# Attention's output product in three fp32r passes, placed ahead of a slot's other projections

## The chip, the cores and the metric

The kernel runs on one core of a Trainium2 chip. The metric is the device time of one execution in microseconds (us). Before the change it is 1490.11 us, the median of three runs (1487.82 to 1490.38).

## What is computed

Eight sequences of 512 rows, 128 columns each, go through a layer in three steps, each on a layer norm of the rows: half a feed-forward, attention, half a feed-forward.

```python
x = x + 0.5 * _L0_ffn_ref(_layernorm(x), ...)
x = x + _L0_attn_ref(_layernorm(x), Wq, Wk, Wv, Wo)
x = x + 0.5 * _L0_ffn_ref(_layernorm(x), ...)
```

Attention has 16 heads of 64 columns, causal:

```python
q = (x @ Wq).reshape(B, S, H, dk)
k = (x @ Wk).reshape(B, S, H, dk)
v = (x @ Wv).reshape(B, S, H, dv)
scores = jnp.einsum('bqhd,bkhd->bhqk', q / math.sqrt(dk), k)
scores = scores + jnp.where(causal, 0.0, -jnp.inf)
attn = jax.nn.softmax(scores, axis=-1)
out = jnp.einsum('bhqk,bkhd->bqhd', attn, v).reshape(B, S, H * dv)
return x + out @ Wo
```

The feed-forward routes each row to 6 of 32 experts (through the best 2 of 4 groups), adds one of 16 anchor experts and a shared one; the kernel computes all hidden columns and scales them by the routing weights.

## The kernel before, in words

**Stages.** A chunk is one sequence: 512 rows, `CH`. The program is `ffn(0)`, `attention()`, `ffn(NC)`, with `NC` = 8 chunks in each. Each engine has its own instruction list, written out by hand in the order in which it stands; semaphores join them. No scheduler moves anything.

**Feed-forward.** A chunk has `HT` = 21 tiles of 128 hidden columns. For each, TensorE makes gate and up (`gate_up`, three fp32r passes each), ScalarE the SiLU (L748), VectorE gate times up (L1124) and the scaling by the routing row (L1156, both inputs in SBUF), and three tiles later TensorE adds the tile's down product in fp32 (L391). `gate_up` of tile j waits for `gated_done` of tile j-3.

**Three passes.** `mm3` (L195 to L199) makes a product of two fp32 operands from their rounded high parts and the rounded rests: high by high, high by low, low by high. The high part comes from a ScalarE copy into an fp32r tile, the low part from a subtraction: on VectorE for activations (`part_lo`), on GpSimd for the weights (`split_lo`, and L1347 for the attention weights `aw`). An ordinary fp32 product is one `matmul` call that the trace records as two matmul instructions.

**Attention.** A pair is two heads; a block has `HP` = 8 pairs, so there are 64 pairs and 64 slots (`attn_slot`). The slot of pair p holds on TensorE, in this order: transposes of the probabilities of pair p-1 (`probT` groups 1 and 2) around the first two score groups of pair p+1; the keys' projection of pair p+2 (`project(..., 1, psA)`), a tile of values (`project_values`), the output product of pair p-2 (`project_out`, L532, fp32), the queries' projection of pair p+2 (`project(..., 0, psA)`); the third score group; the first transposes of pair p; and the product of probabilities and values of pair p-1 (`attend`, L519), again into `psA`. Keys, queries and the attended sums share the PSUM bank `psA`. So the queries' projection waits for `k_lo`, the end of VectorE's low part of the keys, and `attend` waits for `q_lo`.

**ScalarE in a slot:** copy of the attended sums (`ctx_copy`, L825), two copies of transposed probabilities (L814), keys' high part (L781), exponentials of score group 0 (L803), values' copy (L789), queries' high part (L781), exponentials of groups 1 and 2.

**VectorE in a slot:** copy of transposes (L1227), reciprocals (L1220), row maxima of groups 0 and 1 (L1212), keys' low part (L1205), queries' low part (L1201), row maxima of group 2, copy of transposes. GpSimd scales the probabilities after the reciprocals (L1358).

**Slots that carry more.** In blocks 1 to 7: p = 1 has `outT_copy` on ScalarE ahead of the queries' high part and `rows_out` on TensorE after `attend`; p = 2 has `add_out` (L1233) on VectorE between reciprocals and row maxima, and `rows_stats` (L946, L948) between the keys' and the queries' low part; p = 3 has `rows_mean` (L954 to L960) there. The "special" slots (`special_slot`: p = 4 of blocks 0 to 6, and two around the start of the last block) transpose the next block's rows into `psA` first (`a_prep`), and there the keys' projection goes to `psT[:, 1, :]` behind the values, so that nothing waits for `k_lo` ahead of the queries. The output product of a block's pair 0 waits for `out_added`, which `add_out` of the block before sets.

**Start and weights.** SP's queue loads `small` (identity, masks, constants; 992 columns), the first rows, gate weights and bias (L287 to L290), then expert weights. VectorE begins when `consts_loaded` has all three. The attention weights come during the first feed-forward; ScalarE rounds three of them (`attn_split_hi`, tiles 11 to 13 of its last chunk), GpSimd takes the rests, and the first projection waits for `aw_lo`, 3.

## Time and profile before

| what | value |
|---|---|
| median of three runs | 1490.11 us |
| the profiled execution, its own time | 1488.8 us |
| its span, first to last instruction | 1487.0 us |
| granted TensorE clock, mean of the core | 0.998 |
| TensorE busy | 1436.2 us, 97% |
| VectorE busy | 1082.8 us, 73% |
| ScalarE busy | 806.6 us, 54% |
| GpSimd busy | 294.5 us, 20% |
| chain of waits, share by engine | PE 90%, DVE 5%, ACT 3% |
| output product L532 | 128 matmul records of 592 ns |

PE is TensorE's matmuls, PEld its weight loads, DVE is VectorE, ACT is ScalarE, POOL is GpSimd, SP the engine that issues the DMAs. The profiler models the end of a matmul with its pipeline, so consecutive ones overlap in the records: what a matmul costs is read from its start to the next one's start, and not from its duration. The chain of waits follows the work that ended last back to the start; the timeline lists instructions with their start in us from the span's start. Attention runs from about 432 to 1090 us.

### The profile page before, as it was taken

The numbers are of one execution on the slowest core, as the hardware profiler recorded it, in microseconds if no ns is written. First come the engines' busy times: TensorE is split into PE (matmuls) and PEld (weight loads), VectorE is DVE, ScalarE is ACT, GpSimd is POOL, SyncE is SP. The second block draws the span as 40 slices with busy tenths as digits, with TensorE's granted clock in tenths as the row PEclk, the third lists the DMA queues.
The fourth block names the chain that finished last, engine by engine and source line by source line (L and its number), as shares of the span: only waits on it lengthen the run. The fifth ranks groups of instructions, "written<-read, shape, count | busy, mean of one in ns | idle before, by whom it ended". The sixth has DMA issues, their size and how long they took to land.

```text
span 1487.0 us, 28766 instructions
## 1 busy us (share of the span) xinstructions
PE 1436.2 (97%) x9664; PEld 959.0 (64%) x9664; DVE 1082.8 (73%) x2421; ACT 806.6 (54%) x1907; POOL 294.5 (20%) x589
## 2 busy tenths in 40 slices
PE   2999999999988999999999999999899999999998
PEld 1666666666655666666666666666566666666665
DVE  6977877787676666676767677767767877687775
ACT  2443334333356777777777777787644334433422
POOL 2100000000013444434443444344400000000000
PEclk9999999999999999999999999999999999999999
DMA  5343333333310000000000000000033333333332
GB/s 185 128 166 110 104 116 102 111 101 112 114 44 1 2 2 2 2 2 1 2 2 2 2 2 2 1 2 2 2 108 103 117 119 113 104 116 119 111 113 85
DMA packets 58854, 97.80 MB, mean 66 GB/s; under 512 B 6144, under 2 KB 15360, under 8 KB 58752
## 3 DMA queue, kind: packets, MB, share of 16 engines
q1 hardware_dynamic: 58752, 96.44, 20.4%
q8 instruction: 63, 1.03, 0.3%
q14 instruction: 39, 0.32, 0.1%
HBM read 92.75 MB, written 3.67 MB: 65 GB/s over the span
## 4 chain that ended last, share of the span: by engine, by line
PE 90%; DVE 5%; ACT 3%; issue 1%; DMA 1%; POOL 0%; SPq 0%; POOLq 0%; ACTq 0%; DVEq 0%
PE banks L391 19%; PE banks L197 14%; PE banks L199 13%; PE banks L198 13%; PE banks L519 9%; PE banks L484 9%; PE banks L505 5%; PE banks L532 3%; PE banks L494 2%; PE banks L353 2%; ACT work L803 1%; PE banks L363 1%; DVE work L1156 1%; DVE work L1124 1%; DVE q_lo L1201 1%
## 5 line engine op out<-in xcount | busy, mean ns | idle before, releaser
L748 ACT ACTIVATE work<-banks 128x512 f32<-128x512 f32 x336 | 200.6, 598 | 459.1 <-PE banks L199 439.4
L391 PE MATMUL banks<-work,wd 128*128 128x512 f32 x672 | 343.0, 593 | 0.3 <-DVE work L1156 0.3
L1124 DVE TENSOR_TENSOR work<-banks,work 128x512 f32<-128x512 f32 x336 | 231.9, 690 | 150.9 <-ACT work L748 146.0
L803 ACT ACTIVATE work<-banks,nmax 128x512 f32<-128x512 f32 (+3 forms) x512 | 264.0, 527 | 39.0 <-DVE nmax L1212 39.0
L1358 POOL TENSOR_SCALAR work<-work,rrec 128x512 f32<-128x512 f32 (+3 forms) x512 | 262.9, 536 | 0.0
L197 PE MATMUL banks<-xT_hi,wg_hi 128*128 (+1 forms) x336 | 248.3, 739 | 0.1
L1156 DVE TENSOR_TENSOR work<-work 128x512 f32<-128x512 f32 x320 | 226.0, 706 | 15.1 <-DVE work L1124 9.5
L1212 DVE TENSOR_REDUCE nmax<-banks 128x2 f32<-128x1024 f32 (+3 forms) x256 | 198.9, 819 | 10.8 <-PE banks L494 6.6
L1227 DVE COPY stage<-banks 128x1024 f32<-128x1024 f32 (+1 forms) x128 | 122.1, 954 | 59.0 <-PE banks L505 58.9
L391 PEld LDWEIGHTS banks<-work,wd 128*128 128x128 f32 x672 | 126.1, 189 | 34.1 <-DVE work L1156 2.7
L198 PE MATMUL banks<-xT_lo,wg_hi 128*128 (+1 forms) x336 | 133.0, 396 | 0.0
L197 PE MATMUL banks<-xT_hi,wu_hi 128*128 (+1 forms) x336 | 133.0, 396 | 0.0
L199 PE MATMUL banks<-xT_hi,wu_lo 128*128 (+1 forms) x336 | 133.0, 396 | 0.0
L198 PE MATMUL banks<-xT_lo,wu_hi 128*128 (+1 forms) x336 | 132.9, 396 | 0.0
L199 PE MATMUL banks<-xT_hi,wg_lo 128*128 (+1 forms) x336 | 132.9, 396 | 0.0
L814 ACT ACTIVATE stage<-banks 128x512 f32<-128x512 f32 x128 | 76.6, 598 | 86.7 <-PE banks L505 84.6
L505 PE MATMUL banks<-small,work 64*128 64x64 f32 x2560 | 114.7, 225 | 4.3 <-DVE stage L1227 2.7
L505 PEld LDWEIGHTS banks<-small,work 64*128 64x128 f32 x2560 | 98.3, 138 | 17.5 <-issue 16.0
L197 PEld LDWEIGHTS banks<-xT_hi,wg_hi 128*128 128x128 f32 x336 | 64.0, 191 | 67.5 <-issue 64.2
L1201 DVE SCALAR_TENSOR_TENSOR q_lo<-banks,q_hi 128x512 fp32r<-128x512 f32 x64 | 44.3, 693 | 86.8 <-ACT q_hi L781 86.8
L198 PEld LDWEIGHTS banks<-xT_lo,wg_hi 128*128 128x128 f32 x336 | 64.2, 191 | 65.3 <-issue 65.0
L803 ACT ACTIVATION_READ_ACCUMULATOR work<-banks,nmax 128x1 f32 x512 | 105.3, 206 | 0.0
(130 smaller groups left out, 2186.3 us busy)
## 6 DMA issues: line engine op xcount, KB each, us to landing
work<-cw_rows SPq DMA_DIRECT2D x320, 256.0 KB, 3.1
x<-in_x SPq DMA_DIRECT2D x8, 256.0 KB, 6.7
out_rows<-x SPq DMA_DIRECT2D x8, 256.0 KB, 2.2
cw_rows<-cwT SPq DMA_DIRECT2D x16, 96.0 KB, 1.9
stage<-in_w_gate SPq DMA_DIRECT2D x3, 448.0 KB, 5.5
stage<-in_w_up SPq DMA_DIRECT2D x3, 448.0 KB, 6.1
wd<-in_w_down SPq DMA_DIRECT2D x3, 448.0 KB, 6.8
stage<-in_wq SPq DMA_DIRECT2D x1, 512.0 KB, 4.0
```

What stands on the lines that cost most here:

```text
L197: pe.matmul(o, w[0], m[0], start=start, stop=False, skip_group_check=True)
L198: pe.matmul(o, w[0], m[1], start=False, stop=False, skip_group_check=True)
L199: return pe.matmul(o, w[1], m[0], start=False, stop=stop, skip_group_check=True)
L391: pe.matmul(psY, wd[:, j * P:(j + 1) * P], z[part_slot(j)], start=j == 0, stop=j == HT - 1, skip_group_check=True).then_inc(s["down_ps"], 1)
L484: pe.matmul(ps[:, i, o:o + w], qk[0][a][r, p % 2, qb * P:(qb + 1) * P], qk[1][c][r, p % 2, 0:w], start=qb != 0 and k == 0, stop=False, ski ...
L505: m = pe.transpose(psT[:, h, k * DK:(k + 1) * DK], prob[r, p % 2, i, o:o + P], ident[r, h * DK:(h + 1) * DK])
L748: nc.scalar.activation(silu[j % 2], psG[j % 3], ACT.Silu) \
L803: m = nc.scalar.activation(prob[:, p % 2, i, o:o + w], ps[:, i, so:so + w], ACT.Exp, bias=nmax[:, p % 2, i, qb:qb + 1], accum_out=rsum[:, ...
L1124: tt(gated[j % 3], psU[j % 3], silu[j % 2], ALU.mult) \
L1156: tt(z[part_slot(j)], gated[j % 3], spread[:, j % NSPREAD, :], ALU.mult) \
L1212: m = nc.vector.tensor_reduce(nmax[:, p % 2, :, qb], ps[:, :, o:o + (qb + 1) * P], AX.X, ALU.max, negate=True)
L1358: nc.gpsimd.tensor_scalar(t, t, rrec[:, par, i, qb:qb + 1], 1.0, ALU.mult, ALU.mult) \
```

## The change

Four edits. The output weights are a fourth member of `attn_w` and `aw`, rounded and split like the others, and the output product is an `mm3` of them with the attended sums, whose high part ScalarE's copy writes and whose low part is a new VectorE subtraction, `ctx_low`. On TensorE the output product stands ahead of keys and values in every slot; the keys' projection goes to `psT[:, 1, :]` in every slot. On ScalarE the exponentials of group 0 stand ahead of the keys' high part. And `small` is loaded in two parts, the masks' 768 columns as a DMA of their own behind the bias.

```diff
-SMALL = 7 * P + E + TB * G * G
+SMALL = P + E + TB * G * G
...
-            sp.dma_start(small[:, :], small_in).then_inc(s["consts_loaded"], 16)
+            sp.dma_start(small[:, :], small_in[:, 0:SMALL]).then_inc(s["consts_loaded"], 16)
...
+            sp.dma_start(half_f32, small_in[:, SMALL:]).then_inc(s["half_loaded"], 16)
...
-            sp.dma_start(wo[:, :].rearrange("p (j d) -> p j d", d=P),
+            sp.dma_start(attn_w[:, 3, :].rearrange("p (j d) -> p j d", d=P),
...
-                    pe.wait_ge(s["aw_lo"], 3)
+                    pe.wait_ge(s["aw_lo"], 4)
...
             def project_out(b, p, first):
                 n = pair(b, p)
-                pe.wait_ge(s["ctx_sb"], n + 1)
+                pe.wait_ge(s["ctx_lo"], n + 1)
...
-                pe.matmul(psO, wo[:, p * P:(p + 1) * P], ctx_sum[:, :], start=p == 0, stop=p == HP - 1,
-                          skip_group_check=True).then_inc(s["out_ps"], 1)
+                c = slice(p * P, (p + 1) * P)
+                mm3(pe, psO, [w[:, 3, c] for w in aw], [t[:, :] for t in ctx_parts], p == 0, p == HP - 1) \
+                    .then_inc(s["out_ps"], 1)
...
-                    if have_q and special:
+                    if have_q:
                         pe.wait_ge(s["k_lo"], n + 3)
...
-                if have_q and not special:
+                if not (first and p < 2):
+                    bo, po = ahead(b, p, -2)
+                    project_out(bo, po, first)
+                if have_q:
+                    if first and p == 0:
+                        pe.wait_ge(s["q_lo"], 2)
+                    else:
+                        pe.wait_ge(s["pT_act"], 2 * n)
                     if p2 == 0:
                         pe.wait_ge(s["a_xT_lo"], b2 + 1)
-                    project(b2, p2, 1, psA)
+                    project(b2, p2, 1, psT[:, 1, :])
...
                 elif have_q:
-                    pe.wait_ge(s["k_lo"], n + 3)
+                    sums_out()
...
-                    if std_n == 3 and j >= AW_SLOT and j - AW_SLOT < 3:
+                    if std_n == 3 and j >= AW_SLOT and j - AW_SLOT < 4:
                         attn_split_hi(j - AW_SLOT)
...
-                nc.scalar.activation(ctx_sum[:, :], psA, ACT.Copy).then_inc(s["ctx_sb"], 1)
+                nc.scalar.activation(ctx_parts[0][:, :], psA, ACT.Copy).then_inc(s["ctx_hi"], 1)
...
-                if have_q and not special:
-                    part_hi(*ahead(b, p, 2), 1, False)
                 if have_s:
                     exp(*ahead(b, p, 1), 0, first and p == 0)
+                if have_q:
+                    part_hi(*ahead(b, p, 2), 1, False)
...
+            def ctx_low(b, p):
+                n = pair(b, p)
+                dve.wait_ge(s["ctx_hi"], n + 1)
+                tt(ctx_parts[1][:, :], psA, f32(ctx_parts[0][:, :]), ALU.subtract).then_inc(s["ctx_lo"], 1)
...
                     pT_copy(*ahead(b, p, -1), 1, first and p < 3)
+                if not (first and p < 2):
+                    ctx_low(*ahead(b, p, -2))
                 row_rec(b, p)
...
-            for w in range(3):
+            for w in range(4):
                 pool.wait_ge(s["aw_hi"], w + 1)
```

`sums_out` is the wait for the copy of the attended sums (now `ctx_lo` of pair n-2), which stood ahead of the keys in a plain slot and now stands ahead of the queries.

TensorE, the middle of a plain slot (block 4), before. In `xT_hi,aw_hi` the names are the moving and stationary operands in either order; the first three rows are the keys, the next three the values:

```order
L197 MATMUL banks<-xT_hi,aw_hi 128x512
L198 MATMUL banks<-xT_lo,aw_hi 128x512
L199 MATMUL banks<-xT_hi,aw_lo 128x512
L197 MATMUL banks<-aw_hi,xT_hi 128x512
L198 MATMUL banks<-aw_lo,xT_hi 128x512
L199 MATMUL banks<-aw_hi,xT_lo 128x512
L532 MATMUL banks<-ctx_sum,wo 128x512
L197 MATMUL banks<-xT_hi,aw_hi 128x512
L198 MATMUL banks<-xT_lo,aw_hi 128x512
L199 MATMUL banks<-xT_hi,aw_lo 128x512
L484 MATMUL banks<-k_hi,q_hi 128x256 x2
```

The same place in the changed kernel:

```order
L197 MATMUL banks<-ctx_hi,aw_hi 128x512
L198 MATMUL banks<-ctx_lo,aw_hi 128x512
L199 MATMUL banks<-ctx_hi,aw_lo 128x512
L197 MATMUL banks<-xT_hi,aw_hi 128x512
L198 MATMUL banks<-xT_lo,aw_hi 128x512
L199 MATMUL banks<-xT_hi,aw_lo 128x512
L197 MATMUL banks<-aw_hi,xT_hi 128x512
L198 MATMUL banks<-aw_lo,xT_hi 128x512
L199 MATMUL banks<-aw_hi,xT_lo 128x512
L197 MATMUL banks<-xT_hi,aw_hi 128x512
L198 MATMUL banks<-xT_lo,aw_hi 128x512
L199 MATMUL banks<-xT_hi,aw_lo 128x512
```

The output product has moved from behind the values to the front, as three passes in place of one call, and queries follow values at once.

ScalarE, a plain slot from the copy of the attended sums to the queries' high part, before:

```order
L825 ACTIVATE ctx_sum<-banks 128x512
L814 ACTIVATE stage<-banks 128x8x64
L814 ACTIVATE stage<-banks 128x512
L781 ACTIVATE k_hi<-banks 128x512
L803 ACTIVATE work,rsum<-banks,nmax 128x512 x2
L789 ACTIVATE work<-banks 128x512
L781 ACTIVATE q_hi<-banks 128x512
```

and in the changed kernel:

```order
L834 ACTIVATE ctx_hi<-banks 128x512
L823 ACTIVATE stage<-banks 128x8x64
L823 ACTIVATE stage<-banks 128x512
L812 ACTIVATE work,rsum<-banks,nmax 128x512 x2
L790 ACTIVATE k_hi<-banks 128x512
L798 ACTIVATE work<-banks 128x512
L790 ACTIVATE q_hi<-banks 128x512
```

The keys' high part and the two exponentials have changed places; the queries' high part keeps its place behind them all.

VectorE, the start of a plain slot in the changed kernel; the second row is new, the others stand as before:

```order
L1233 COPY stage<-banks 128x8x64
L1238 TENSOR_TENSOR ctx_lo<-banks,ctx_hi 128x512
L1226 RECIPROCAL rrec<-rsum 128x8
L1218 TENSOR_REDUCE nmax<-banks 128x2 x2
L1211 TENSOR_TENSOR k_lo<-banks,k_hi 128x512
L1207 SCALAR_TENSOR_TENSOR q_lo<-banks,q_hi 128x512
```

One subtraction more stands ahead of the reciprocals and the row maxima in each slot.

## Rows read from the trace of the kernel before

**Rows 1.** Windows: stretch, its length, busy us (x instructions) by engine, clock, DMA.

```profile
530.00:1065.00 535.00, 532.33 (x5627) 350.58 (x5625) 378.64 (x656) 414.64 (x1203) 230.79 (x487) 1.00 0.01 2
```

**Rows 2.** Timeline, TensorE, one plain slot: start, us, engine, line, operation.

```profile
767.94 0.50 PE L197 MATMUL banks<-xT_hi,aw_hi 128*128 128x512 f32 x1
...
768.75 0.46 PE L197 MATMUL banks<-aw_hi,xT_hi 128*128 128x512 f32 x1
...
769.50 1.02 PE L532 MATMUL banks<-ctx_sum,wo 128*128 128x512 f32 x2
770.32 0.50 PE L197 MATMUL banks<-xT_hi,aw_hi 128*128 128x512 f32 x1
...
771.22 0.39 PE L484 MATMUL banks<-k_hi,q_hi 64*128 64x256 f32 x2
...
772.86 2.37 PE L519 MATMUL banks<-stage,values 128*64 128x512 f32 x16
```

**Rows 3.** Timeline, TensorE, a special slot: rows' transposes, values, output product, queries.

```profile
807.60 0.66 PE L353 MATMUL banks<-small,xn 128*128 128x128 f32 x4
808.36 0.50 PE L197 MATMUL banks<-aw_hi,xT_hi 128*128 128x512 f32 x1
...
809.87 1.02 PE L532 MATMUL banks<-ctx_sum,wo 128*128 128x512 f32 x2
...
810.96 0.39 PE L198 MATMUL banks<-xT_lo,aw_hi 128*128 128x512 f32 x1
```

**Rows 4.** Timeline, ScalarE, the same plain slot.

```profile
768.05 0.60 ACT L814 ACTIVATE stage<-banks 128x512 f32<-128x512 f32 x1 [1.23 <-PE banks L505]
768.95 0.60 ACT L781 ACTIVATE k_hi<-banks 128x512 fp32r<-128x512 f32 x1 [0.29 <-PE banks L199]
769.44 0.68 ACT L803 ACTIVATE work<-banks,nmax 128x512 f32<-128x512 f32 x1
...
770.77 0.60 ACT L789 ACTIVATE work<-banks 128x512 f32<-128x512 f32 x1
```

**Rows 5.** Timeline, VectorE, the same plain slot.

```profile
766.23 0.69 DVE L1227 COPY stage<-banks 128x512 f32<-128x512 f32 x1 [1.20 <-PE banks L505]
766.84 0.19 DVE L1220 RECIPROCAL rrec<-rsum 128x8 f32<-128x8 f32 x1
767.11 2.09 DVE L1212 TENSOR_REDUCE nmax<-banks 128x2 f32<-128x1024 f32 x2
769.58 0.69 DVE L1205 TENSOR_TENSOR k_lo<-banks,k_hi 128x512 fp32r<-128x512 f32 x1 [0.38 <-ACT k_hi L781]
```

**Rows 6.** Timeline, VectorE, from slots p = 2 and p = 3.

```profile
787.20 0.64 DVE L1233 TENSOR_TENSOR x<-x,banks 128x512 f32<-128x512 f32 x1
...
790.52 0.86 DVE L948 BATCH_NORM_STATS2 bn<-x 128x6 f32<-128x128 f32 x4
...
800.14 0.14 DVE L954 COPY pace<-small 128x1 f32<-128x1 f32 x1
...
800.92 0.16 DVE L960 TENSOR_SCALAR var_eps<-mean_var 128x4 f32<-128x4 f32 x1
```

**Rows 7.** Timeline, VectorE and GpSimd, last chunk of the first feed-forward.

```profile
417.31 2.05 DVE L1156 TENSOR_TENSOR work<-work 128x512 f32<-128x512 f32 x1
...
420.00 0.69 DVE L1156 TENSOR_TENSOR work<-work 128x512 f32<-128x512 f32 x1
...
416.14 2.67 POOL L1347 TENSOR_TENSOR aw_lo<-stage,aw_hi 128x1024 fp32r<-128x1024 f32 x1 [0.48 <-ACT aw_hi L768]
```

**Rows 8.** First piece of the chain of waits; DMA issue: count, KB, us to landing.

```profile
2.23 4.84 DMA bias<-in_gate_bias
...
small<-in_small SPq DMA_DIRECT2D x1, 496.0 KB, 3.2
```

**Rows 9.** Waits of TensorE, all of the run: us in total, times, longest.

```profile
PE banks L197 <- DVE k_lo L1205: 1.9, 3, 0.7
PE banks L519 <- DVE q_lo L1201: 1.4, 7, 0.2
```

More of the change, by code:

```diff
@@ L248, in special_slot, with part_source @@
             return next_rows(b, p) or ffn_rows(b, p) or ffn_logits(b, p)
+        def part_source(which, early):
+            return psT[:, 1 - which, :] if early else psT[:, 1, :] if which else psA
         def ahead(b, p, d):
@@ L579, in attn_slot, with sums_out @@
                     probT(*ahead(b, p, -1), 2)
-                if first and p == 0:
-                    pe.wait_ge(s["v_sb"], 3)
-                elif first and p == 1:
-                    pe.wait_ge(s["q_lo"], 3)
-                else:
-                    pe.wait_ge(s["ctx_sb"], n - 1)
+                def sums_out():
+                    if first and p == 0:
+                        pe.wait_ge(s["v_sb"], 3)
+                    elif first and p == 1:
+                        pe.wait_ge(s["q_lo"], 3)
+                    else:
+                        pe.wait_ge(s["ctx_lo"], n - 1)
+                if special:
+                    sums_out()
                 if next_rows(b, p):
@@ L608, in attn_slot @@
                 if have_q and special:
-                    if not have_v:
-                        pe.wait_ge(s["pT_act"], 2 * n)
-                    project(b2, p2, 1, psT[:, 1, :])
-                if not (first and p < 2):
-                    bo, po = ahead(b, p, -2)
-                    project_out(bo, po, first)
-                if have_q and special:
                     if next_rows(b, p):
@@ L773, in a_xT_high, with part_hi @@
                     .then_inc(s["a_xT_hi"], 1)
-            def part_hi(b, p, which, early, special=False):
+            def part_hi(b, p, which, early):
                 n = pair(b, p)
@@ L780, in part_hi @@
                     act.wait_ge(s["s_ps"], 3 * n - 3)
[L781 removed]
+                nc.scalar.activation(qk[which][0][:, p % 2, :], part_source(which, early),
                                      ACT.Copy, scale=(float(DK) ** -0.5, 1.0)[which]) \
@@ L1192, in a_xT_low, with part_lo @@
                     .then_inc(s["a_xT_lo"], 1)
-            def part_lo(b, p, which, early, special=False):
+            def part_lo(b, p, which, early):
                 n = pair(b, p)
@@ L1198, in part_lo @@
                 hi, lo = [t[:, p % 2, :] for t in qk[which]]
-                ps = psT[:, 1 - which, :] if early else psT[:, 1, :] if special else psA
+                ps = part_source(which, early)
                 if which == 0:
@@ L1313, in _ @@
             normalise(0, "xn_ready")
-            nc.vector.tensor_copy(half[:, :], small[:, P:7 * P])
+            dve.wait_ge(s["half_loaded"], 16)
+            nc.vector.tensor_copy(half[:, :], half_f32)
             nc.vector.memset(cw[:, :, ROWS:], 0.0)
```

31 lines of the change are left out of this document (16 added, 15 removed).

## The prediction

> **What bounds the kernel.** I read the windows first: in the middle of attention TensorE is busy 532.33 of 535.00 us at the full clock, VectorE 378.64, ScalarE 414.64, and DMA 1% [rows 1]. TensorE is the bound there, and what a change costs is read from the spacing of its starts. The second view is its timeline in one plain slot [rows 2]. Keys take 0.81 us (767.94 to 768.75), values 0.75, the fp32 output product 0.82 (to 770.32), queries 0.90 (to 771.22), and `attend` begins at 772.86. The third is what the others do meanwhile [rows 4, 5], since the change puts an instruction on VectorE and turns ScalarE's order round: both have idle time, but the end of `q_lo` is needed by `attend`, and it is the end of a chain through both.
>
> **Part 1, the product on TensorE.** In a plain slot the queries start at 770.32, the moment `k_lo` ends (769.58 + 0.69 = 770.27, and 0.05 on the way) [rows 2, 5]. In a special slot nothing waits for `k_lo`, and output product plus the queries' first pass take 810.96 - 809.87 = 1.09 [rows 3], against about 1.16 here (0.82, and 0.34 for a first pass). The wait costs 0.07. Three fp32r passes take 0.70: 0.81 for the keys less 0.11, which the first pass after transposes loses to its weight load, and which the product, now first, takes over from the keys. Values at 0.75 contain 0.05 of waiting for ScalarE's second copy of transposes (768.05 + 0.60) [rows 4]; now the keys wait for it and the product covers it exactly as the keys did. A plain slot is then 0.81 (product) + 0.75 (keys) + 0.70 (values) + 0.80 (queries, with 0.10 for the step to 64-row weights) = 3.06, in place of 3.28: **-0.22 us**, if nobody else is late.
>
> The Trainium skill ("TensorE: Matmul & The Clock Gate", section Back-to-back issue gap) gives 512 columns a spacing of 216 ns alone and 131 ns sustained in a stream. By these, three passes would be 0.65 or 0.39 us and the slot's gain 0.27 or 0.53. The trace has 0.23 to 0.24 a pass, so the sum goes by that.
>
> **Part 2, is anyone late in a plain slot?** `ctx_low` reads one PSUM and one SBUF operand, as `k_lo` does: 0.69, of which 0.61 shifts what follows (766.23 to 766.84) [rows 5]. It starts at 766.84 and ends at 767.53. The product wants it at 767.94: 0.4 to spare. The reciprocals begin at 767.45, the first maximum at 767.56; it has 1024 of the 1792 elements of the two, 1.2 of 2.09 us [rows 5], and ends at 768.76. The exponentials begin at 768.80 (before: 769.44) and take 1.33 to the next ScalarE instruction [rows 4]. Keys' high part: 770.13. At 0.49 for a copy (768.95 to 769.44), values 770.62, queries' high part 771.11 (their projection ends at 770.90, and 0.2 later ScalarE can read it, as with the keys: 768.75 and 768.95). The low part begins 0.63 after the high one, as for the keys [rows 4, 5]: 771.74, ends 772.43, `attend` may start at 772.48. TensorE arrives at 772.86 - 0.22 = 772.64. So **0.16 us to spare**, and -0.22 stands. `k_lo` ends at 771.45, ahead of the masks' second half at about 771.9, which waits for it now.
>
> **Part 3, the slots that carry more.**
> p = 2, seven of them. The reciprocals were at about 787.09, `add_out` at 787.20 [rows 6]; it moves to 787.81, the maximum to 788.36, the exponentials to 789.60, keys' high part 790.93, `k_lo` 791.56, the statistics from 792.17 to 793.09 (0.86 and a short copy), `q_lo` to 793.74. `attend` stood 6.02 after the reciprocals, as in rows 2 and 5: at 793.11. It moves to 793.78: **+0.67**. (The product of pair 0 now also waits for `add_out`, to 788.5, some 0.3 late; that hides behind the same wait.)
> p = 3, seven: 0.94 of means stands between `k_lo` and `q_lo` (800.14 to 801.08) [rows 6]. On the plain clock `q_lo` starts at 771.37 + 0.94 = 772.31 and `attend` at 773.05: **+0.2**.
> p = 1, seven: `attend` already waits 0.2 for `q_lo` [rows 9]; ScalarE's chain reaches the queries' high part 0.15 earlier: **-0.15**.
> Special, eight: the product is 0.15 cheaper (0.85 of the 1.09, against 0.70), and it fills a hole. The rows' transposes are issued by about 808.1 (807.60 + 0.66, less what the last record overlaps), the values start at 808.36, when ScalarE's second copy is done [rows 3]: 0.3. Together **-0.44**.
> The first three slots: two of the three long waits for `k_lo` [rows 9] go, 1.3 us, and in slot 2 the exponentials come sooner: **-1.9** together. Slot 5 of the last block loses the third wait: -0.85. Slots 6 and 7 there have no projections as cover: +0.26 for later exponentials, +0.61 because GpSimd starts that much later and nothing covers it. Tail -0.3, slot 0 of the last block -0.2, slot 3 of the first 0.
> Plain: 27 x -0.22 = -5.9. Attention: -5.9 + 4.7 + 1.4 - 1.05 - 3.5 - 1.9 - 0.85 + 0.87 - 0.5 = **-6.7**.
>
> **Part 4, before attention.** A fourth rest on GpSimd. While the third runs (416.14 to 418.81) a VectorE product of two SBUF operands takes 2.05 instead of 0.69, ending 0.55 after it [rows 7]. The fourth starts at once behind, and runs to about 421.7; the next such product (420.00) ends at 422.3 instead of 420.69. VectorE is full from there to the low part of attention's first rows, for which the first projection waits: **+1.5**, between 0 (a fourth operation that meets none) and +2.4 (the first product shut out as well).
> The Trainium skill ("SBUF — State Buffer", section Who interferes with whom) says that a `tensor_tensor` with both inputs in SBUF and a GpSimd operation shut each other out for a whole instruction; it doesn't say who goes first when both have waited. The trace agrees with the first; by the other answer the term is +2.4, my upper end.
>
> The start: VectorE begins when the bias has landed, 2.23 + 4.84 = 7.07 [rows 8], behind 496 KB of `small` and 256 KB of rows. 384 KB less stand ahead of it now. If bytes set the pace, 384/496 of `small`'s 3.2 us to landing [rows 8] is the most they can be worth, 2.5. If the bias lands as long after its issue as `small` did, it is there at 5.4, 1.6 sooner. If it is late by itself, nothing is gained. I take **-2.0**, between the first two, and 0 and -2.5 as ends; routing and the first tiles hang on VectorE, so it is kept. The masks are first wanted 4 us later, and their DMA ends about when the bias did.
> The Trainium skill ("DMA: Bandwidth & Descriptors", section Anatomy of one DMA) gives 2.0 us fixed plus the bytes: the bias at 4.3, a gain of 2.7, and the sum 0.7 lower. No run here shows it alone.
>
> **Sum.** -2.0 + 1.5 - 6.7 = -7.2 us: a span of 1479.8, an execution of 1481.6 against its own 1488.8, which is 1.3 under the median of the runs shown; against that median of 1490.11, **1482.9**.
>
> **Rivals.**
> A, slower. The low part of the attended sums makes `q_lo` late in every slot. For: it stands ahead of the maxima, everything to `q_lo` is one chain now, and I have 0.16 to spare. If the chain is L late over my reckoning, the 27 plain slots lose L - 0.16 and the other 29 about L: 56 L - 4.3. From L = 0.21 the gain is gone, from 0.26 it is over 3 us slower; at L = 0.35 it costs 15.3, 1498. Against: the instructions' durations are those of rows 4 and 5, and none is new in form. Chance 0.10.
> B, TensorE alone decides; the added VectorE work in p = 2 and 3 finds room, because ScalarE or VectorE overlap more than I let them. Fourteen slots at -0.22 in place of +0.67 and +0.22: -9.2, 1473.7. Against: the order is fixed. Chance 0.10.
> C, the parts ahead of attention bring nothing: the bias lands late by itself (its packets are small) and the fourth rest costs 2.4. -6.7 + 2.4 + 0 = -4.3, 1485.8. Chance 0.20.
> D, the change in passes is no gain: a pass of the product costs more than one of the projections, because its operand has just been written. Then 0.82 stays and only the waits go: -7.2 + 54 x 0.12 = -0.7, 1489.4. Little speaks for it. Chance 0.05.
> Forecast: 0.55.
>
> **How the numbers follow.** A measurement of this kernel tells 0.2%, 3 us, from no change: faster is under 1487.1. The forecast, less 0.03 for its upper edge, B and most of C (0.17) are faster (0.79), the rest of these, D and a weak A are the same (0.12), A beyond L = 0.26 is slower (0.09). B and A, 0.2, are left out but for their near parts; C, D and the ends of the two terms of part 4 are in: 1477.5 to 1489.
>
> **What would show it.** The product as three passes 0.23 apart right after the transposes, plain slots of 9.48 us in place of 9.70 (start of `attend` to the next), no wait of L197 for `k_lo`, waits of `attend` for `q_lo` of 0.9 us in p = 2 and 0.45 in p = 3 and none in plain slots; VectorE's first instruction near 5.1 instead of 7.08; a second stretched L1156 near 420. It would be wrong if plain slots too show a wait for `q_lo`, if the product waits for `ctx_lo`, or if the granted clock falls in attention.

## The result, and the profile after

The changed kernel takes **1481.77 us** (median of 8 runs, 1479.59 to 1485.13) beside 1489.41 for the kernel before on the same chip (8 runs): ratio **0.9951**, 95% interval 0.9938 to 0.9964, so 7.3 us faster by the ratio (7.6 by the difference of the two medians). The profiled execution took 1480.01 us with a span of 1478.2, against 1488.8 and 1487.0: 8.8 less of span, where 7.2 were forecast.

The page after: busy time by engine, and the middle of attention as in [rows 1].

```profile
PE 1422.5 (96%) x9728; PEld 974.7 (66%) x9728; DVE 1111.0 (75%) x2485; ACT 803.0 (54%) x1908; POOL 297.4 (20%) x590
530.00:1065.00 535.00, 524.35 (x5748) 367.02 (x5746) 407.33 (x728) 415.33 (x1220) 234.49 (x493) 1.00 0.01 2
```

VectorE's share rose (378.64 to 407.33 us in this stretch), and TensorE's gaps grew: 10.65 us of 535 in place of 2.67. Some 3 us of the 10.65 are waits of the last two slots, which now come early enough to fall into the stretch (before, they lay behind 1065). Most of the rest is in two lines of the waits (us in total, times, longest):

```profile
PE banks L524 <- DVE q_lo L1207: 5.2, 15, 0.5
...
PE banks L197 <- DVE x L1244: 2.1, 7, 0.3
```

Both lines are new in kind or size: `attend` (L524) waits for `q_lo`, and the output product waits for `add_out` (L1244). The waits of L197 for `k_lo` [rows 9] are gone.

**A plain slot**, TensorE, as in [rows 2]:

```profile
761.50 0.50 PE L197 MATMUL banks<-ctx_hi,aw_hi 128*128 128x512 f32 x1
...
762.30 0.46 PE L197 MATMUL banks<-xT_hi,aw_hi 128*128 128x512 f32 x1
...
763.07 0.40 PE L197 MATMUL banks<-aw_hi,xT_hi 128*128 128x512 f32 x1
...
763.76 0.39 PE L197 MATMUL banks<-xT_hi,aw_hi 128*128 128x512 f32 x1
...
764.55 0.38 PE L489 MATMUL banks<-k_hi,q_hi 64*128 64x256 f32 x2
...
766.18 2.37 PE L524 MATMUL banks<-stage,values 128*64 128x512 f32 x16
```

Product 0.80, keys 0.77, values 0.69, queries 0.79: 3.05, where 3.28 stood. No matmul row shows a wait. Only the keys' weight load does, for ScalarE's second copy of transposes, as Part 1 had said; the product stands ahead of it and fills nearly all of that time:

```profile
762.26 0.19 PEld L197 LDWEIGHTS banks<-xT_hi,aw_hi 128*128 128x128 f32 x1 [0.24 <-ACT stage L823]
```

The other two engines in the same slot, as in [rows 4] and [rows 5]:

```profile
761.62 0.60 ACT L823 ACTIVATE stage<-banks 128x512 f32<-128x512 f32 x1 [1.24 <-PE banks L510]
762.30 0.69 ACT L812 ACTIVATE work<-banks,nmax 128x512 f32<-128x512 f32 x1
...
763.64 0.60 ACT L790 ACTIVATE k_hi<-banks 128x512 fp32r<-128x512 f32 x1
...
764.66 0.60 ACT L790 ACTIVATE q_hi<-banks 128x512 fp32r<-128x512 f32 x1
```

```profile
760.38 0.68 DVE L1238 TENSOR_TENSOR ctx_lo<-banks,ctx_hi 128x512 fp32r<-128x512 f32 x1
760.98 0.19 DVE L1226 RECIPROCAL rrec<-rsum 128x8 f32<-128x8 f32 x1
761.09 2.04 DVE L1218 TENSOR_REDUCE nmax<-banks 128x2 f32<-128x1024 f32 x2
764.27 0.69 DVE L1211 TENSOR_TENSOR k_lo<-banks,k_hi 128x512 fp32r<-128x512 f32 x1 [1.14 <-ACT k_hi L790]
765.29 0.69 DVE L1207 SCALAR_TENSOR_TENSOR q_lo<-banks,q_hi 128x512 fp32r<-128x512 f32 x1 [0.33 <-ACT q_hi L790]
```

`q_lo` ends at 765.98 and `attend` starts at 766.18: the chain has 0.2 to spare. Note the bracket on `k_lo`: VectorE stands idle for 1.14 us there. It matters in the two slots below.

**Slot p = 2**, VectorE, then TensorE:

```profile
780.90 0.64 DVE L1244 TENSOR_TENSOR x<-x,banks 128x512 f32<-128x512 f32 x1
781.45 2.09 DVE L1218 TENSOR_REDUCE nmax<-banks 128x2 f32<-128x1024 f32 x2
784.67 0.69 DVE L1211 TENSOR_TENSOR k_lo<-banks,k_hi 128x512 fp32r<-128x512 f32 x1 [1.14 <-ACT k_hi L790]
...
785.35 0.86 DVE L954 BATCH_NORM_STATS2 bn<-x 128x6 f32<-128x128 f32 x4
786.12 0.67 DVE L1207 SCALAR_TENSOR_TENSOR q_lo<-banks,q_hi 128x512 fp32r<-128x512 f32 x1
```

```profile
781.68 0.47 PE L197 MATMUL banks<-ctx_hi,aw_hi 128*128 128x512 f32 x1 [0.30 <-DVE x L1244]
...
786.85 2.37 PE L524 MATMUL banks<-stage,work 128*64 128x512 f32 x16 [0.50 <-DVE q_lo L1207]
```

TensorE waits twice, 0.30 and 0.50. I had said that the first hides behind the second. It does in the sum, since the slot grew by no more than was told, but it is a lateness of its own that stays when the second is gone (e8).

**Slot p = 3**, VectorE, then TensorE:

```profile
795.07 0.37 DVE L962 BATCH_NORM_AGGREGATE mean_var<-bn 128x2 f32<-128x6 f32 x4
795.48 0.21 DVE L965 COPY mean<-mean_var 128x4 f32<-128x4 f32 x1
...
795.66 0.68 DVE L1207 SCALAR_TENSOR_TENSOR q_lo<-banks,q_hi 128x512 fp32r<-128x512 f32 x1
```

```profile
796.40 1.08 PE L524 MATMUL banks<-stage,work 128*64 128x512 f32 x4
```

**Ahead of attention, and its start**: VectorE's first instruction, the two stretched products, GpSimd's third and fourth operation, TensorE's first projection.

```profile
6.29 0.15 DVE L952 COPY pace<-small 128x1 f32<-128x1 f32 x1 [6.29 <-DMA bias<-in_gate_bias]
416.52 2.07 DVE L1162 TENSOR_TENSOR work<-work 128x512 f32<-128x512 f32 x1
419.22 2.16 DVE L1162 TENSOR_TENSOR work<-work 128x512 f32<-128x512 f32 x1
415.35 5.48 POOL L1363 TENSOR_TENSOR aw_lo<-stage,aw_hi 128x1024 fp32r<-128x1024 f32 x2 [0.48 <-ACT aw_hi L777]
432.22 0.50 PE L197 MATMUL banks<-xT_hi,aw_hi 128*128 128x512 f32 x1 [0.54 <-DVE xT_lo L1197]
```

The first projection stood at 431.76 before. The next rows' transposes, at the end of attention, stand at 1082.28 and stood at 1091.10: all of the 8.8 us is there by then, and attention itself went from 659.34 to 650.06.

### The profile page after: what moved, and what is told of

Read it like the earlier page. It is cut to its first block, busy times and chain, and to the rows that moved or that the text cites. A ratio compares the mean times of both kernels' runs of the same rounds, so it can differ in the third digit from the quotient of the medians.

```text
span 1478.2 us, 29011 instructions
## 1 busy us (share of the span) xinstructions
PE 1422.5 (96%) x9728; PEld 974.7 (66%) x9728; DVE 1111.0 (75%) x2485; ACT 803.0 (54%) x1908; POOL 297.4 (20%) x590
## 4 chain that ended last, share of the span: by engine, by line
PE 82%; DVE 10%; ACT 4%; issue 3%; DMA 1%; POOL 0%; SPq 0%; POOLq 0%; DVEq 0%; ACTq 0%
PE banks L396 18%; PE banks L197 13%; PE banks L199 13%; PE banks L198 13%; PE banks L524 10%; PE banks L489 7%; PE banks L510 5%; PE banks L358 2%; DVE nmax L1218 2%; PE banks L499 1%; ACT work L812 1%; DVE work L1130 1%; DVE work L1162 1%; PE banks L368 1%; DVE q_lo L1207 1%
## 5 line engine op out<-in xcount | busy, mean ns | idle before, releaser
L197 PE MATMUL banks<-xT_hi,wg_hi 128*128 (+1 forms) x336 | 247.7, 737 | 0.1
L1218 DVE TENSOR_REDUCE nmax<-banks 128x2 f32<-128x1024 f32 (+3 forms) x256 | 195.8, 807 | 6.4 <-PE banks L499 6.3
L197 PE MATMUL banks<-xT_hi,wu_hi 128*128 (+1 forms) x336 | 133.0, 396 | 0.0
L197 PEld LDWEIGHTS banks<-xT_hi,wg_hi 128*128 128x128 f32 x336 | 64.0, 191 | 67.5 <-issue 63.8
L489 PE MATMUL banks<-k_hi,q_hi 64*128 64x256 f32 (+2 forms) x512 | 101.3, 391 | 2.4 <-ACT work L812 1.7
```

Of the source, the lines that this page charges most:

```text
L197: pe.matmul(o, w[0], m[0], start=start, stop=False, skip_group_check=True)
L489: pe.matmul(ps[:, i, o:o + w], qk[0][a][r, p % 2, qb * P:(qb + 1) * P], qk[1][c][r, p % 2, 0:w], start=qb != 0 and k == 0, stop=False, ski ...
L1218: m = nc.vector.tensor_reduce(nmax[:, p % 2, :, qb], ps[:, :, o:o + (qb + 1) * P], AX.X, ALU.max, negate=True)
```

## The experiments

Each is an edit of the changed kernel; e2 and e11 are the order of the change without its passes. A slot's length is the distance of two first score products (`k_hi,q_hi`, 512 columns), and all slots of a kind agree within 0.03:

```
us a slot  before  after    e1     e2     e3     e4     e5     e8    e12
plain        9.70   9.47   9.57   9.57  10.24  10.16   9.87   9.47   9.46
p = 1       10.56  10.35  10.35  10.26  11.31  10.74  10.93  10.35  10.05
p = 2        9.70  10.32  10.32   9.73  10.51  10.33  10.92   9.87   9.47
p = 3        9.69   9.55   9.57   9.56  10.24  10.16  10.12   9.47   9.46
p = 4       10.34   9.79   9.96   9.96  10.57   9.79  10.18   9.80   9.80
```

### e1: one fp32 product in the same place

```diff
-                mm3(pe, psO, [w[:, 3, c] for w in aw], [t[:, :] for t in ctx_parts], ...)
+                pe.matmul(psO, f32(aw[0][:, 3, c]), f32(ctx_parts[0][:, :]), ...)
```

> The changed kernel, but the output product is one fp32 matmul again, in the same place, from the high parts alone (the low part of the attended sums and of the weight are still computed and waited for, and left out of the product). Theory (TensorE sets the spacing, a pass of the product costs 0.23): the product takes 0.82 in place of 0.70 us, 56 times, +6.7; in the seven p = 2 slots it hides behind the wait of attend for q_lo. About +5.8 over the changed kernel's 1480.0: 1485.8, 0.998 of before, plain slots of 9.58 instead of 9.46. Rival D (the passes are no gain): plain slots stay at 9.46 and the time at 1480.

Measured: 1487.54 us, ratio 0.9983 (0.9974 to 0.9992). The span of the profiled execution is 1482.8, 4.6 over the changed kernel's; that execution is the fastest of eleven, and the medians differ by 5.8, as expected. Plain slots are 0.10 longer, special ones 0.17, p = 1 and p = 2 not at all, since they wait for VectorE. So three passes are cheaper than one fp32 product here too, and D falls. Where the 0.10 lies is another matter:

```profile
763.30 0.19 PEld L197 LDWEIGHTS banks<-xT_hi,aw_hi 128*128 128x128 f32 x1 [0.46 <-ACT stage L823]
762.54 1.12 PE L538 MATMUL banks<-ctx_hi,aw_hi 128*128 128x512 f32 x2
763.30 0.60 PE L197 MATMUL banks<-xT_hi,aw_hi 128*128 128x512 f32 x1
763.74 0.40 PE L198 MATMUL banks<-xT_lo,aw_hi 128*128 128x512 f32 x1
```

By the starts the product takes 0.76, less than three passes (0.80), and the first pass behind it 0.44 in place of 0.30. But this boundary says little, because the keys' weight load waits for ScalarE's copy in both kernels (0.46 here, 0.24 in the changed kernel), and the first pass is recorded from the start of that load (763.30 in both rows). In a special slot, where the copy is done by then, the same two distances are 0.46 and 0.64, against 0.78 and 0.23 with three passes. Only the sum of product and next first pass can be compared: 1.20 against 1.10 in a plain slot. How much of the 0.10 belongs to which of the two, the rows don't tell.

### e2: the order alone

```diff
-        aw = [sb(f"aw_{n}", [P, 4, H * DK], F32R) for n in ("hi", "lo")]
+        aw = [sb(f"aw_{n}", [P, 3, H * DK], F32R) for n in ("hi", "lo")]
+        wo = sb("wo", [P, H * DK])
+        ctx_sum = sb("ctx_sum", [P, CH])
...
-                if not (first and p < 2):
-                    ctx_low(*ahead(b, p, -2))
...
-            for w in range(4):
+            for w in range(3):
```

> Only the order of the change: output product in fp32 from one copy of the sums, in front of the projections, keys into the second bank of transposes, exponentials ahead of the keys' rounding; no low part on VectorE, no fourth rounded weight. Theory (the chain through VectorE and ScalarE to q_lo sets p = 2, TensorE the others): plain slots 9.58 (+0.12 against the changed kernel), p = 2 slots 9.71 (-0.61), first projection of attention 1.25 sooner. About +5.9 - 4.3 - 1.25 = +0.4: 1480.4 to 1481, no different from the changed kernel, so that the passes bring nothing net. Rival (the low part and the fourth weight are hidden work): +6.5, 1486.5, p = 2 slots at 10.3 still.

Measured: **1477.91 us, ratio 0.9919** (0.9906 to 0.9933), outside the interval of the whole change (0.9938 to 0.9964). Plain and p = 2 slots came as expected (9.57, 9.73), and the first projection stands at 430.81, 1.41 sooner, 0.12 of it from an earlier start. It ended some 3 us under the forecast, and its span, 1473.8, is 4.4 under the changed kernel's where +0.4 was expected. About 2.5 us of this miss are in the slots. The expectation put +0.12 on every slot but p = 2, and the table has 0.10 in plain ones, 0.01 in p = 3 and -0.09 in p = 1, where the low part had been late too. Another 2.1 are behind the last score product. The last two slots have no projections as cover, and TensorE's wait for GpSimd is 1.60 there, not 2.15: 0.6. The other 1.5 come from TensorE keeping its full clock in the last slot, where the changed kernel did not; that part may be chance. Without it the changed kernel's passes still cost 2.9 us more than they bring: 1.3 ahead of attention, 1.0 in the slots and 0.6 in the last two. So half of the change brings more than the whole: **the passes as they were made cost more than they bring.**

### e3: keys rounded ahead of the exponentials

```diff
-                if have_s:
-                    exp(*ahead(b, p, 1), 0, first and p == 0)
                 if have_q:
                     part_hi(*ahead(b, p, 2), 1, False)
+                if have_s:
+                    exp(*ahead(b, p, 1), 0, first and p == 0)
```

> The changed kernel, but ScalarE rounds the keys ahead of the exponentials of the first score group again. Theory (one chain): the keys' rounding can begin at 763.27 on the clock of the plain slot at 759.5 to 769, the exponentials then start at 763.76 instead of 762.30, q_lo ends 0.9 late and attend starts 0.75 later: 54 slots x 0.75 = +40, 1520. Rival (nothing on TensorE waits for k_lo before the masks, so ScalarE's order is free): 1480, plain slots 9.46.

Measured: 1527.37 us (one run), plain slots 10.24, 0.77 longer, as the chain was reckoned. But it is not `q_lo` that TensorE waits for:

```profile
789.87 0.39 PE L489 MATMUL banks<-k_hi,q_hi 64*128 64x256 f32 x2 [0.64 <-ACT work L812]
```

The third score group goes into the bank that the exponentials of the first read, so lateness on ScalarE meets TensorE there, before it meets `attend`. So the new order on ScalarE is what makes the new order on TensorE possible: keys are projected one product later, and a ScalarE that waits for them is late with all else. Whether it would gain anything with the old order on TensorE, no run tried.

### e4: product behind keys and values

```diff
-                if not (first and p < 2):
+                if special and not (first and p < 2):
                     bo, po = ahead(b, p, -2)
                     project_out(bo, po, first)
...
+                if not special and not (first and p < 2):
+                    bo, po = ahead(b, p, -2)
+                    project_out(bo, po, first)
```

> The changed kernel, but in the slots that are not special the three passes of the output product stand behind the keys' and values' projections, where the product was before; the keys still go into the second bank of transposes. Theory (the gain of the order is that the queries no longer wait for k_lo, and that comes from the keys' bank, not from the product's place): plain slots 9.46 to 9.51, the time 1480 to 1482.5; in p = 2 the wait for add_out goes and the wait for q_lo grows by as much. Rival (the place in front is what covers the wait): plain slots 9.58, 1485.5.

Measured: 1507.33 us, ratio 1.012 (1.0104 to 1.0135). Both expectations fall, mine most:

```profile
786.30 0.50 PE L197 MATMUL banks<-xT_hi,aw_hi 128*128 128x512 f32 x1 [0.69 <-ACT stage L826]
```

In 52 slots the keys wait 0.69 us for ScalarE's second copy of transposes (L826 here), since the keys now go into the bank that this copy reads. Before, they went into `psA`, which was free. So the keys' new bank and the product's new place belong together: the product, with a bank of its own, is work that can fill the time of that copy.

### e5: the low part twice, and the masks ahead of the bias

```diff
+                if n < NC * HP - 2:
+                    tt(spare, psA, f32(ctx_parts[0][:, :]), ALU.subtract).then_inc(s["ctx_free"], 1)
...
             sp.dma_start(small[:, :], small_in[:, 0:SMALL]).then_inc(s["consts_loaded"], 16)
+            sp.dma_start(half_f32, small_in[:, SMALL:]).then_inc(s["half_loaded"], 16)
```

> The changed kernel with two edits at different ends. First, VectorE makes the low part of the attended sums a second time, into a tile that nobody reads; the output product waits for the first, the queries' bank is free after the second (0.61 us more on VectorE ahead of the maxima, 62 times). Theory (one chain, 0.15 us to spare in a plain slot): plain slots 9.46 + 0.61 - 0.15 = 9.92, p = 2 slots 10.32 + 0.61 = 10.93, p = 3 slots about 10.1, attention some 29 us longer: about 1508. Rival (VectorE is idle a quarter of the time, so it has room): plain slots 9.46. Second, the 384 KB of masks are issued right behind the small constants, so that 496 KB stand ahead of the bias again. If bytes ahead set the bias's landing, VectorE starts at 7.1 to 7.5 instead of 6.29; if the bias is late by itself, at 6.3 to 6.8 (its issue moves by 0.5).

Measured: 1513.49 us (one run). Plain slots grew by 0.40, p = 1, p = 2 and p = 3 by 0.58 to 0.60. What a slot doesn't show of 0.60 was to spare: **0.2 in a plain slot, nothing in the three others.** Rival A had the right mechanism; it needed 0.2 more on the chain. The start:

```profile
8.86 0.15 DVE L953 COPY pace<-small 128x1 f32<-128x1 f32 x1 [8.86 <-DMA bias<-in_gate_bias]
```

With the masks ahead the bias lands 2.6 us later than after the change, 0.5 of it because it is issued later (2.70 in place of 2.22). Bytes ahead of it count; but the same 496 KB as one DMA gave 7.08 before, so this may not be bytes alone, and it lies beyond both expectations. It is one profile.

### e7: GpSimd's fourth subtraction later

```diff
                 pool.wait_ge(s["aw_hi"], w + 1)
+                if w == 3:
+                    pool.wait_ge(s["a_xT_lo"], 1)
```

> The changed kernel, but GpSimd's fourth subtraction (the rest of the output weight) waits until VectorE has made the low part of attention's first rows, and the output product waits for it. Theory (the fourth one stretches a product on VectorE from 0.69 to 2.16, and VectorE is full from there): no stretched product near 419, attention's first projection at about 430.9 instead of 432.22, the span 1.3 shorter, 1476.9. Rival (that stretch is covered): first projection at 432.2, span 1478.2.

```profile
417.28 2.05 DVE L1163 TENSOR_TENSOR work<-work 128x512 f32<-128x512 f32 x1
419.97 0.69 DVE L1163 TENSOR_TENSOR work<-work 128x512 f32<-128x512 f32 x1
```

The second stretched product is gone. From VectorE's first instruction to the first projection it is 424.65 us (7.08 to 431.73), 424.68 before and 425.93 after: the fourth subtraction costs **1.27** (1.1 to 1.3 over all pairs of kernels with and without it). Yet the kernel takes 1481.14 us, ratio 0.9939 (0.9926 to 0.9953), the same as without the edit. In the profiled execution, the slowest of its five, the gain is lost in the first slots, to the clock: windows of 10 us from 440 of this kernel, then of the changed one (clock third from the end).

```profile
450.00:460.00 10.00, 7.68 (x85) 6.12 (x85) 8.24 (x22) 6.90 (x21) 1.54 (x4) 0.84 0.01 2
460.00:470.00 10.00, 9.70 (x85) 6.68 (x87) 4.98 (x9) 7.64 (x23) 2.73 (x6) 0.78 0.00 0
```

```profile
450.00:460.00 10.00, 7.54 (x91) 5.87 (x89) 7.98 (x22) 7.17 (x21) 1.17 (x4) 0.91 0.01 2
460.00:470.00 10.00, 9.28 (x103) 6.53 (x104) 7.05 (x13) 8.68 (x25) 3.91 (x9) 1.00 0.00 0
```

The other executions show both sides of it. At mean granted clocks of 0.997, 0.996 and 0.995 this kernel's spans are 1477.3, 1478.3 and 1479.4, and the changed kernel's are 1478.2, 1479.5 and 1480.4. At the same clock the edit seems worth about 1 us, which the clock takes back. (The clock is given to 0.001, which leaves some 0.7 us of a span open.)

### e8: statistics ahead of the keys' low part

```diff
+                if p == 2 and not first:
+                    dve.wait_ge(s["out_added"], b)
+                    rows_stats(b - 1)
+                if p == 3 and not first:
+                    rows_mean(b - 1, b - 1 + 2 * NC)
                 if have_q:
                     part_lo(*ahead(b, p, 2), 1, False)
-                if p == 2 and not first:
...
```

> The changed kernel, but in p = 2 and p = 3 the rows' statistics and means stand ahead of the keys' low part, in the 1.14 us in which VectorE waits for ScalarE, and no longer between the two low parts. Theory (the statistics are what makes q_lo late in p = 2): attend's wait of 0.50 for q_lo goes, p = 2 slots 9.82, p = 3 slots 9.46, seven times 0.50 + 0.08 = -4.1, span 1474.1. Rival (q_lo is late in p = 2 because of add_out ahead of the maxima, and the statistics only fill its wait): p = 2 slots stay near 10.3, or longer if the keys' low part now waits for the statistics.

Measured: **1477.92 us, ratio 0.9922** (0.9909 to 0.9936), span 1475.2. The statistics fill the idle time, and the wait for `q_lo` in p = 2 is gone:

```profile
782.38 0.87 DVE L954 BATCH_NORM_STATS2 bn<-x 128x6 f32<-128x128 f32 x4
783.54 0.69 DVE L1211 TENSOR_TENSOR k_lo<-banks,k_hi 128x512 fp32r<-128x512 f32 x1 [0.30 <-ACT k_hi L790]
784.52 0.69 DVE L1207 SCALAR_TENSOR_TENSOR q_lo<-banks,q_hi 128x512 fp32r<-128x512 f32 x1 [0.29 <-ACT q_hi L790]
```

Slots p = 2 are 9.87, p = 3 9.47. The rival falls. What is left in p = 2, 0.40 over a plain slot, starts with the product's wait for `add_out`, still 0.30.

### e9: the bias on a semaphore of its own

```diff
-            dve.wait_ge(s["consts_loaded"], 48)
+            dve.wait_ge(s["consts_loaded"], 32)
...
+            dve.wait_ge(s["bias_loaded"], 16)
             for k in ROUTING:
```

> The changed kernel, but the bias's DMA has a semaphore of its own, waited for only ahead of the routing. Theory (VectorE's first instruction waits for the bias alone, and the kernel's start hangs on VectorE): it starts when rows and gate weight have landed, between 4.1 and 5.3 instead of 6.29, and the span is 1 to 2.2 shorter. Rival (something later in the first tiles, the weights' loads or their rounding, sets the start): VectorE starts sooner and the span stays within 0.3 of 1478.2.

```profile
4.22 0.15 DVE L952 COPY pace<-small 128x1 f32<-128x1 f32 x1 [4.22 <-DMA gate_w<-in_gate_weight]
```

VectorE starts 2.07 sooner and the first projection stands at 430.13, 2.09 sooner: the start hangs on VectorE. The span is 1476.9, 1.3 shorter (the first slots took 0.7 longer in this profile); 1478.24 us, ratio 0.9924 (0.9911 to 0.9938). The bias, 16 KB, is late for another reason than what is issued ahead of it: all of that has landed by 4.22, and the bias lands near 6.5. Whether that is due to its own form or to the masks and expert weights issued behind it, no run tells apart.

### e10 to e13: everything together

e10 has the edits of e7, e8 and e9 and two more: `add_out` at the head of p = 2, where VectorE waits 1.13 us for transposes, and in p = 1 ScalarE's copy of the rows (`outT_copy`) behind the queries' high part.

```diff
+                if p == 2 and not first:
+                    add_out(b - 1)
                 if not (first and p < 1):
                     pT_copy(*ahead(b, p, -1), 1, first and p < 3)
...
                 if have_q:
                     part_hi(*ahead(b, p, 2), 0, False)
+                if p == 1 and not first:
+                    outT_copy(b - 1)
```

e11 is e2 with these edits, e12 is e10 without the edit of e7, and e13 is e10 again.

> The changed kernel with its three late chains undone: GpSimd's fourth subtraction after the low part of attention's first rows, the bias on a semaphore of its own, and in the slots statistics and means ahead of the keys' low part, add_out at the head of p = 2 (VectorE is idle there for 1.13 us before its copy of transposes), and the rows' last copy on ScalarE in p = 1 behind the queries' high part. Theory (in these slots TensorE is late only because of what stands ahead of it on the other two engines, by the waits seen: 0.30 + 0.11 in p = 2 for add_out, 0.23 in p = 1 for q_lo): slots p = 1 10.12, p = 2 and p = 3 9.46, plain 9.46; start -2.1, fourth rest -1.27, attention -3.7 - 2.9 - 1.7: span about 1466.5, give or take 1.7 for where the clock falls. Rival (these waits hide others just behind, normalisation on GpSimd or a bank that is not free): p = 2 stays at 9.8, and the span above 1470.

> The order of the change alone (output product in fp32, no low part on VectorE, no fourth rounded weight) with the same edits to the slots and the bias. Theory: plain, p = 2 and p = 3 slots 9.57, p = 1 10.25, special 9.96; start -2.1 and p = 2 7 x -0.15 against the order alone: span about 1470.5, so that three passes are worth 3 to 4 us once nothing is late for them. Rival (the passes are worth nothing in any arrangement): as short as the kernel with all edits and three passes.

> The kernel with all edits, but GpSimd's fourth subtraction stands directly behind the third again. Theory (the fourth one costs 1.27 us ahead of attention and nothing else hangs on it): first projection of attention 1.27 later than in the kernel with all edits beside it (about 430.3 against 429.0), and the time about 1.3 longer, 1472.1 against 1470.8. Rival (the edit is paid back in the first slots: both kernels that had it showed TensorE at 1.2 GHz for longer there, 13.7 and 10.2 us against 3.4 to 6.8 in the others): TensorE at half clock for about 6.8 us here, and the time the same or shorter, 1469 to 1470.8.

> The kernel with all edits once more, unchanged, beside the one above: 1470.8, and if half-clock time in the first slots belongs to the later subtraction, 10 us of it or more again; if it falls by chance, any of 3.4, 6.8 or 10.2.

```
                               us     ratio   95% interval      span   at 1.2 GHz: first slots, last two
e10, all edits            1470.80    0.9875   0.9859 to 0.9892  1469.2   10.2    6.8
e11, order alone + edits  1473.76    0.9896   0.9879 to 0.9912  1471.8    6.8    3.4
e12, all but e7's edit    1468.02    0.9859   0.9839 to 0.9878  1466.0    6.8    0.0
e13, e10 again            1470.64    0.9864   0.9840 to 0.9887  1469.7   13.7    6.8
changed kernel            1481.77    0.9951   0.9938 to 0.9964  1478.2    6.8    3.4
```

(The last two columns, in us, are worked out from the granted clock of windows of 1 us, 430 to 480 and 1035 to 1090.) p = 2 and p = 3 slots are as short as plain ones, and p = 1 is 10.05, 0.07 less than I had asked. In e12 VectorE adds the rows in what was idle time:

```profile
772.88 0.69 DVE L1244 TENSOR_TENSOR x<-x,banks 128x512 f32<-128x512 f32 x1 [0.62 <-PE banks L358]
773.53 0.69 DVE L1233 COPY stage<-banks 128x512 f32<-128x512 f32 x1
```

TensorE's waits for `q_lo` are down to two, 0.6 and 0.2 us, from sixteen in the changed kernel, and none in a slot is for `add_out`. e12 beats both kernels: 1.4% under before, 0.9% under the change. Against e11, e10 shows three passes beat one fp32 product by 3 us once nothing is late for them. The intervals of e10 and e11 overlap, but the four runs of each, on one chip, do not (1470.53 to 1471.63 and 1473.37 to 1474.61), and neither do the slots (9.47 to 9.57, 9.80 to 9.96). The stretch from the first slots to the last score product is 5.6 us shorter in e10's profile. The span is only 2.6 shorter, because e10 lost 1.4 in the first slots and 1.6 at the end, where together it spent 6.8 us more at half clock. On the later subtraction the rival's side is the nearer: the three profiles with it (e7, e10, e13) show TensorE at half clock for 10.2 to 13.7 us of the first slots, all others 3.4 to 6.8, and e12 is no slower without it (the intervals overlap). That it causes the longer stretches is not shown. One execution of e13 kept a mean clock of 0.998, which is e12's, and had a span of 1465.1, less than any of e12 (1466.0 at least). So the later subtraction does not always bring the longer stretches, and where the clock is the same it seems to pay about 1 us. In the median it did not pay.

## Why the prediction was right, point by point

**The number.** 1482.9 forecast, 1481.8 measured, well inside the range. That it is so near is in part luck. Attention gained 9.3 us where 6.7 were told, and the two terms ahead of it cost 0.5 where they were to bring 0.5; p = 3 alone is 2.4 better than told, the start and slots 6 and 7 together 2.4 worse. Between the two profiles the gain is 8.8, not 7.2. The terms, in us (a kernel's TensorE times from the slots above):

```
term                                   predicted   measured
start                                     -2.0       -0.8
fourth subtraction on GpSimd              +1.5       +1.27
27 plain slots                            -5.9       -6.2
p = 1, seven                              -1.05      -1.5
p = 2, seven                              +4.7       +4.3
p = 3, seven                              +1.4       -1.0
special, eight                            -3.5       -4.1
first three slots                         -1.9       -2.0
slot 5 of the last block                  -0.85      -0.64
its slots 6 and 7                         +0.87      +2.1
tail and slot 0 of the last block         -0.5       -0.2 in slot 0
```

- **Part 1 held**: -0.23 a plain slot where -0.22 was reckoned. e1 and e2 split it: 0.10 for the passes and 0.13 for the order, where I had 0.12 and 0.10. Of the signs named, slots of 9.48, no wait of L197 for `k_lo`, none for `q_lo` in plain slots and a second stretched product near 420 all came. By the Trainium skill ("TensorE: Matmul & The Clock Gate", Back-to-back issue gap) a pass would be 0.13 sustained; all rows here keep to 0.23, and the measurement decides.
- **Part 2 held**: 0.16 to spare by reckoning, 0.2 by e5. The chain is as was told, though its first meeting with TensorE is the third score group (e3), which I did not name; had the exponentials been 0.8 later, TensorE would have waited there.
- **p = 2 held in size** (+0.62 for +0.67). The waits are 0.50 for `q_lo` and 0.30 for the product, where one of 0.9 was told. e8 and e10 take its two causes away in turn, 0.45 for the statistics and then 0.40 for `add_out`. The prediction said the first sets it alone; with it gone, the second still holds the slot. `add_out` moved alone was not run.
- **p = 3 has the wrong sign.** The step that failed is "0.94 of means stands between `k_lo` and `q_lo`". After the change it is 0.65 (795.01 to 795.66): the small copy of the means, 0.40 before, took 0.21, and `q_lo` started 0.06 behind the start of the last one (795.60). [Rows 6] gave the ends of a stretch with nothing queued behind it: `q_lo` came 0.84 later there. `attend` waits 0.1 now, not 0.45. What the copy's 0.40 was stays open: GpSimd was normalising beside it in both kernels.
- **The start is the term that was mis-sized**: -2.0 taken, -0.8 between the two profiles (7.08 and 6.29). Six more kernels with the same first DMAs say how loose that is: VectorE began at 6.24, 6.17, 6.56, 5.88, 7.08 and 6.58 in e1, e2, e3, e4, e7 and e8, a mean of 6.4 with the changed kernel. Before has a single profile, and its 7.08 is no later than e7's. The bound by bytes was the right kind (e5: 2.6 for 384 KB put back), and so was a lateness that these bytes don't explain (e9); I took a point too near one end. The Trainium skill's sum ("DMA: Bandwidth & Descriptors", Anatomy of one DMA) is stated there for DMAs that GpSimd issues; carried over to this one, which SP issues, it puts the bias at 4.3 by my estimate. The trace does not agree: VectorE waits for it until 6.29.
- **The fourth subtraction held**: 1.27 for 1.5, nearly the same in every pair of kernels (e2, e7). The trace agrees with the Trainium skill's rule ("SBUF — State Buffer", Who interferes with whom) that a VectorE instruction with two SBUF inputs and a GpSimd one that reads SBUF shut each other out: 2.16 in place of 0.69. On who goes first when both wait, the rows add that VectorE got in between GpSimd's operations: its product ran from 416.52 to 418.59, GpSimd's third subtraction ended at 418.03, and the fourth took 2.83 in place of 2.39.
- **Slots 6 and 7 of the last block** cost more than told, 1.5 of it because TensorE ran transposes and `attend` at half clock. In e12, with the same waits at full clock (0.71 and 2.37 for these two rows), they cost +0.6. The prediction had named a fall of the granted clock in attention as a sign against it; these 3.4 us at half clock, which the kernel before does not have there, are the step it left out:

```profile
1066.29 1.12 PE L510 MATMUL banks<-small,work 64*128 64x64 f32 x16 [2.15 <-POOL work L1374]
1067.34 3.46 PE L524 MATMUL banks<-stage,values 128*64 128x512 f32 x16
```

- **The rivals.** A falls at 0.2 to spare (e5). B's slots p = 2 and p = 3 came half true, p = 3 at once, p = 2 only with e10. C was half right on the start and wrong on the fourth subtraction. D falls with e1. None of them was what e2 shows, that one part of the change, the passes, does not pay. I had most of its prices, 54 slots at 0.12 against 1.5 ahead of attention and 4.7 in the p = 2 slots, and never set them against each other.

## What to carry to other kernels

Cost each part of a change against leaving that part out, not only the sum against before: here the order alone was worth 0.8%, the whole 0.5%, and the passes paid (3 us) only after the work they displaced on VectorE had been moved into idle time. An instruction that stands between two links of a chain and needs neither belongs into the wait ahead of the chain; the bracket with the idle time shows the place (1.14 us for 0.86 of statistics, 1.13 for 0.69 of `add_out`). When an operand's bank is changed, look up who reads that bank last: the new bank of the keys cost 0.69 us a slot wherever no other work stood in front of it.

## What the runs showed of the hardware

- The granted clock falls to one half in stretches around TensorE's waits, in the first slots of attention and in its last two, and how many such stretches a kernel gets decides more than some of the edits. In the changed kernel TensorE had waited 0.79 and 2.15 us in the last two slots before it ran at half clock (3.46 us for an `attend` of 2.38); in e2 it had waited 0.79 and 1.60, and the clock stayed up (2.37). It is no rule that these runs settle: e11 has e2's waits and spent 3.4 us at half clock, and e12 has the changed kernel's waits and kept its full clock.
- An fp32 product of 128x512 and the first fp32r pass behind it take 1.20 us together, three fp32r passes and the next one 1.10 (e1 and the changed kernel, plain slots). Single starts within such a group can shift by 0.3 with what the next weight load waits for, so they are no price of one instruction.
- The landing of one small DMA at the start varies by 1.2 us from profile to profile (5.86 to 7.05 over twelve profiles that issue it at 2.2) with the same DMAs ahead of it. A term of that size can't be read from one profile.
